# Router steps moved to the beginning of the pair two further on, and the residual additions of attention made by GpSimd, in a cross-attention and mixture-of-experts kernel

## The chip, the cores and the metric

The kernel runs on one core of one Trainium2 chip. Its time is the device time of one execution in microseconds (us). Three runs of the kernel before gave 643.98, 644.26 and 647.44 us; the median is 644.26 us. One more execution was profiled: 646.02 us, of which 644.2 us is the span from the first to the last instruction.

A core has five engines, each of which works through its own list of instructions in order: TensorE (PE), VectorE (DVE), ScalarE (ACT), GpSimd (POOL) and SyncE (SP, which here only starts DMAs). They wait for one another by semaphores. An instruction that waits holds back everything behind it on its engine.

## What is computed

```python
# 16 sequences of 128 tokens, width 256, 16 heads of 16
x = x + xattn(layernorm(x), ctx, ctx, pad_mask, causal_mask, Wq, Wk, Wv)
x = x + ffn(layernorm(x))

def ffn(x):                                   # 2048 tokens
    ys = geglu(x @ Ws1 + bs1) @ Ws2 + bs2     # shared expert, all tokens
    logits = (x @ Wr + br) / 1.5              # router, 12 experts
    top_val, top_idx = top_k(logits, 2)       # two experts for each token
    w = softmax(top_val)
    yr = sum over the two of w * (geglu(x @ We1[e] + be1[e]) @ We2[e] + be2[e])
    return ys + yr
```

## The kernel before

**Two phases.** The 16 sequences are treated in 8 pairs (0 to 7); the attention of these pairs fills the first 200 us or so. Then come the shared expert and the routed experts, in 43 slots of 128 tokens. Between them GpSimd scatters the normalised tokens to the rows of their experts (`scatter`, 32 indirect DMAs, two for each of 16 token tiles) and converts the first expert's weights.

**A pair on TensorE.** For each of a pair's two sequences (b = 0, 1) there is one *score burst* (`scores`, lines 568 and 574: the mask, then q times k), which fills the PSUM tile `ps_s`. The burst of sequence 0 of pair p+1 stands at the end of pair p (`next_scores`), that of sequence 1 in the middle of a pair. VectorE takes every burst in two halves ("units"): a maximum (`softmax_max`, line 1317), then a subtraction out of `ps_s` (`softmax_add`, line 1324). The next burst waits until all units of the one before are subtracted (`shifted`). ScalarE makes the exponentials, TensorE transposes them in four groups per sequence (`prob_transposes`, line 585), ScalarE copies each group, and TensorE multiplies by the values (`values`, line 595). Then ScalarE copies the result (`out_copy`), TensorE transposes it back (`out_transposes`, line 603), and VectorE divides it (`norm`, into the tile `att`) and adds it to `x_all` (`residual`, line 1348). `residual` also takes the statistics of the second layer norm.

**Steps.** Between these pieces stand the *steps* of other pairs, each of which goes through one of two PSUM banks in turn (`ps_x` and a half of `ps_t`): `k`, `q`, `v` (the projections of the next pair), `xT` (transposes of the normalised x two pairs on), `r` and `l` (the router of pair p-1: transposes of the second layer norm's output `xn2p`, line 488, and the product with the router's weights, line 539), and `n` (the ranks of tokens within their experts, for the first 8 tiles). The steps have one numbering over all pairs (`order`, `index_of`); a step on TensorE waits until the one two before it is taken out of its bank (`xb_free`), and `l` waits until ScalarE has copied `r`. VectorE makes the low halves of `k`, `q` and `xT` and takes out `l`.

**The second layer norm.** After the residual of sequence 1, GpSimd computes 1/sqrt of the variance (`rstd`), VectorE makes `xn2p` (`ln2_apply`, line 1364), SyncE saves it (`save_xn2`), and TensorE's step `r` reads it, all of it in the pair after the one that it belongs to.

**GpSimd** normalises x for pair p+2 (`normalise_x`), splits the context for pair p+2 into two parts (`split_ctx`), and in pairs 1 to 4 converts the shared expert's weights. **SyncE** loads the context, saves `xn2p` and fills the rows of the experts with zeros (`fill`, 8 DMAs of 3.3 MB). The scatters wait for all fills, for `xn2p` of the first four pairs and for the row numbers of the first 8 tiles (`rows_ready`).

**Line numbers** are those of the kernel before. The rows of the changed kernel in the section on the change have its own numbering (line 585 has become 595, and so on).

Of the kernel before, what the change touches and what calls it, by code (L numbers as in the profile page):

```python
# [18 lines left out]
B, S, D = 16, 128, 256  # L19
# [33 lines left out]
def build(nc, x_d, ctx_d, pad_d, sub_d, wq_d, wk_d, wv_d, bias_d, bst_d, tab_d, ws1_d, ws2_d, w1_d,  # L53
# [260 lines left out]
    def order(p, first, last):  # L314

        if last:
            return ["r", "l", "n"]
        if first:
            return ["xT", "k", "q", "v", "xT"]
        if isinstance(p, int) and p == PAIRS - 2:  # L320
            return ["k", "q", "n", "v", "r", "l"]
        return ["k", "q", "v", "xT", "r", "l"]

    def base_of(p, first):

        return len(FIRST) if first else 6 * p + len(FIRST) - 1
# [15 lines left out]
    def each_pair(eng, body):  # L342

        body(0, 0, True, False)
        with eng.Fori(0, (PAIRS - 4) // 2) as i:
            body(i * 2 + 1, 1, False, False)
            body(i * 2 + 2, 0, False, False)
        body(PAIRS - 3, 1, False, False)
        body(PAIRS - 2, 0, False, False)
        body(PAIRS - 1, 1, False, True)  # L350
# [23 lines left out]
    with block:  # L374
# [3 lines left out]
        def _(sp):  # L378
# [50 lines left out]
            def pair(p, first):  # L429

                sp.wait_ge(c_split, p + 2)
                load_ctx(p + 2)
                if not first:
                    save_xn2(p - 1)
                fill(p + 1)
# [4 lines left out]
            sp.wait_ge(c_split, PAIRS - 1)  # L440
            load_ctx(PAIRS - 1)
# [41 lines left out]
        def _(pe):  # L483
# [180 lines left out]
            def pair(p, par, first, last):  # L664
# [5 lines left out]
                def put(s, parts=(0, 1), again=False):  # L670

                    if s not in todo:
                        return
                    idx, bank = index_of(s, p, first, last, again), bank_of(s, p, first, last, again)
                    if s == "n":
                        rank_step(idx, bank, batch_in(p))
                    elif s in ("r", "l"):
                        router(s, p - 1, idx, bank, index_of("r", p, first, last) + 1)
                    else:
                        step(s, p + (2 if s == "xT" and (again or not first) else 1), 1 - par, idx, bank, parts=parts)  # L680
# [15 lines left out]
                else:  # L696
                    prev = p * 2 - 1
                    prob_transposes(prev, 0)
                    put("k", (0,))
                    prob_transposes(prev, 1)  # L700
# [11 lines left out]
                    put("n")  # L712
# [238 lines left out]
        def _(sc):  # L951
# [82 lines left out]
            def pair(p, par, first, last):  # L1034
# [5 lines left out]
                def put(s, again=False):  # L1040
# [4 lines left out]
                    if s == "r":  # L1045
                        router(s, idx, bank)
                    else:
                        step(s, 1 - par, idx, bank)
# [7 lines left out]
                else:  # L1056
                    prev = p * 2 - 1
                    prob_copy(prev, 0)
# [4 lines left out]
                    exp(p * 4, 0)  # L1063
                    out_copy(prev)
                    put("q")
# [6 lines left out]
                put("xT", first)  # L1072
                prob_copy(cur, 3)
                put("r")
# [4 lines left out]
                exp(p * 4 + 3, 3)  # L1079

# [127 lines left out]
        def _(ve):  # L1208
# [125 lines left out]
            def norm(p, b):  # L1334
# [4 lines left out]
                ve.wait_ge(nstep, (p * 2 + b) * 2 + 1)  # L1339
                vec.tensor_tensor(att[:, :].rearrange("p (h d) -> p h d", d=HD), o[:, :, 0:HD],  # L1340
# [3 lines left out]
            def residual(p, b):  # L1344
# [3 lines left out]
                vec.tensor_tensor(xs, xs, att[:, :], ALU.add).then_inc(added, 1)  # L1348
                ve.wait_ge(added, p * 2 + b + 1)
# [101 lines left out]
            def pair(p, par, first, last):  # L1451
# [5 lines left out]
                def put(s, again=False):  # L1457
# [6 lines left out]
                    elif s in ("r", "l"):  # L1464
                        router(s, p - 1, idx, bank)
# [13 lines left out]
                else:  # L1479
                    softmax_add(p * 4, 0)  # L1480
# [8 lines left out]
                    put("q")  # L1489
# [7 lines left out]
                softmax_max(p * 4 + 3, 3, p * 2 + 1)  # L1497
                if not first:
                    ln2_apply(p - 1)
                softmax_add(p * 4 + 3, 3)  # L1500
                put("xT", first)
                norm(p, 0)
                residual(p, 0)
                if first:
                    ve.wait_ge(x_rest_in, 16)
                    ve.wait_ge(router_in, 32)
                    ln1_stats(3)
                put("l")
                softmax_max(p * 4 + 4, 0, p * 2 + 2)
                if isinstance(p, int) and p == PAIRS - 3:  # L1510
                    choose(1, 0)
# [285 lines left out]
        def _(gp):  # L1797
# [55 lines left out]

            def first_step(s, q):
# [63 lines left out]
            split_ctx(2)  # L1918
            for p in range(1, PAIRS - 1):
# [11 lines left out]
                if p == 4:  # L1931
# [3 lines left out]
                    load_raw2(0)  # L1935

# [149 lines left out]
```

## Time and profile before

| | |
|---|---|
| median of three runs | 644.26 us |
| profiled execution | 646.02 us |
| its span | 644.2 us |
| PE busy | 582.1 us (90% of the span) |
| DVE busy | 447.1 us (69%) |
| ACT busy | 282.6 us (44%) |
| POOL busy | 364.5 us (57%) |
| mean granted TensorE clock | 0.954 of full speed |

Busy shares are averages over both phases. In the rows of the section further down, times are us from the span's start; a timeline row gives start, duration, engine, line, operation, output and inputs, and in brackets the idle time before it with the engine and line that ended it. The granted clock is given as a share of 2.4 GHz; it has two levels, 1.00 and 0.50.

### The profile page before, as it was taken

To read this page: it belongs to the slowest core of one execution; us is meant where nothing else is said; L and a number is where in the kernel's file an instruction comes from. 1 tells how busy PE (TensorE), PEld (TensorE's weight loads), DVE (VectorE), ACT (ScalarE), POOL (GpSimd) and SP (SyncE) were. 2 spreads that over 40 slices of the span, in tenths; PEclk is the share of its full clock that TensorE was granted. 3 is DMA by queue.
4 is the path that set the end of the run, shared out by engine and by line. 5 is a ranking of instruction groups with operands and counts; after the bars stand their busy time and mean duration, and the time that the engine had idled before them with its cause. 6 is when DMAs were issued, how large, how long until landed. Compare 5 with 4: busy or idle time off the path is not lost.

```text
span 644.2 us, 14068 instructions
## 1 busy us (share of the span) xinstructions
PE 582.1 (90%) x4092; PEld 479.8 (74%) x4093; DVE 447.1 (69%) x976; ACT 282.6 (44%) x629; POOL 364.5 (57%) x419
## 2 busy tenths in 40 slices
PE   7597979879788778799999999999999999999995
PEld 6465757656556777587887888878887888889995
DVE  5588668577678867667766677766676776665767
ACT  3255536454356623344444444444444444444432
POOL 3533151452108878699983886778886684000773
PEclk9799879789799989799999999999999999999998
DMA  9940651628651432364535365263465241110443
GB/s 289 395 173 31 216 185 61 244 99 292 227 214 68 172 140 91 122 225 156 204 136 179 95 222 188 81 228 130 144 222 183 86 131 33 33 34 18 139 134 121
DMA packets 47620, 98.91 MB, mean 154 GB/s; under 512 B 4449, under 2 KB 23521, under 8 KB 47585
## 3 DMA queue, kind: packets, MB, share of 16 engines
q1 hardware_dynamic: 36192, 50.41, 22.5%
q0 software_dynamic: 10976, 47.72, 22.2%
q10 hardware_dynamic: 416, 0.33, 0.2%
q8 instruction: 21, 0.34, 0.2%
q14 instruction: 15, 0.11, 0.1%
HBM read 57.15 MB, written 39.19 MB: 150 GB/s over the span
## 4 chain that ended last, share of the span: by engine, by line
PE 72%; DVE 12%; issue 5%; POOL 5%; ACT 3%; SPq 2%; DMA 1%; DVEq 0%; ACTq 0%; POOLq 0%
PE ps_s L790 29%; PE ps_o L823 9%; PE ps_o L824 5%; PE ps_s L752 4%; PE ps_t L800 3%; PE ps_t L585 3%; PE ps_s L568 2%; POOL rows_in L1913 2%; PE ps_s L574 2%; DVE prob L1324 2%; PE ps_x L510 2%; PE ps_t L510 2%; DVE nmax L1317 1%; PE ps_s L800 1%; PE ps_x L539 1%
## 5 line engine op out<-in xcount | busy, mean ns | idle before, releaser
L790 PE MATMUL ps_s<-ring,xTh 128*128 (+1 forms) x516 | 153.4, 419 | 0.5 <-DVE xTl L1638 0.5
L790 PEld LDWEIGHTS ps_s<-ring,xTh 128*128 128x128 f32 x516 | 89.2, 191 | 14.6 <-DVE xTl L1638 0.8
L1624 DVE TENSOR_TENSOR ag<-ps_s,up_bias 128x512 f32<-128x512 f32 x129 | 89.1, 691 | 12.1 <-PE ps_s L790 7.4
L823 PE MATMUL ps_o<-ring,hTh 128*128 x258 | 96.0, 410 | 0.8 <-issue 0.8
L1814 POOL TENSOR_TENSOR ring<-stage,ring 128x512 fp32r<-128x512 f32 x76 | 95.7, 1292 | 1.1
L790 PE MATMUL ps_s<-ring,xTl 128*128 (+1 forms) x258 | 81.0, 395 | 0.0
L824 PE MATMUL ps_o<-ring,hTl 128*128 x258 | 72.3, 280 | 0.0
L1800 POOL TENSOR_TENSOR ve<-mv,eps 128x2 f32<-128x2 f32 x16 | 3.5, 216 | 116.9 <-DVE mv L1356 100.6
L2025 POOL DMA_INDIRECT gath<-rows_out,idx_out x32 | 31.0, 968 | 65.8 <-DMA rows_out<-y_row 56.3
L1629 DVE TENSOR_TENSOR ag<-ag,ps_s 128x256 f32<-128x256 f32 x129 | 54.3, 421 | 16.0 <-ACT ps_s L1105 0.5
L1105 ACT ACTIVATE ps_s<-ag 128x256 f32<-128x256 f32 x129 | 50.2, 389 | 32.4 <-DVE ag L1624 31.0
L980 ACT ACTIVATE probT<-ps_t 128x512 f32<-128x512 f32 x64 | 37.8, 597 | 52.4 <-PE ps_t L585 51.2
L790 PEld LDWEIGHTS ps_s<-ring,xTl 128*128 128x128 f32 x258 | 48.8, 189 | 11.4
L1113 ACT ACTIVATE hTh<-ps_t 128x256 fp32r<-128x256 f32 x86 | 33.1, 385 | 53.6 <-PE ps_t L800 53.6
L1647 DVE TENSOR_TENSOR y_row<-ps_o,y_lo 128x256 f32<-128x256 f32 x43 | 18.3, 425 | 55.0 <-ACT y_lo L1128 55.0
L823 PEld LDWEIGHTS ps_o<-ring,hTh 128*128 128x128 f32 x258 | 48.5, 188 | 10.6 <-issue 1.0
L1827 POOL TENSOR_TENSOR ring<-stage,ring 128x512 fp32r<-128x512 f32 x40 | 51.0, 1300 | 1.2
L1633 DVE TENSOR_TENSOR hTl<-ps_t,hTh 128x256 fp32r<-128x256 f32 x86 | 36.1, 420 | 21.5 <-issue 16.8
L824 PEld LDWEIGHTS ps_o<-ring,hTl 128*128 128x128 f32 x258 | 48.9, 189 | 0.0
L1324 DVE TENSOR_TENSOR prob<-ps_s,nmax 128x1024 f32<-128x1024 f32 x32 | 39.1, 1221 | 13.2 <-PE ps_t L585 12.9
L752 PE MATMUL ps_s<-xgh,ring 128*128 128x256 f32 x256 | 47.4, 292 | 0.3
L1317 DVE TENSOR_REDUCE nmax<-ps_s 128x8 f32<-128x1024 f32 x32 | 38.9, 1217 | 10.3 <-PE ps_s L574 8.7
(254 smaller groups left out, 1290.1 us busy)
## 6 DMA issues: line engine op xcount, KB each, us to landing
rows_in<-y_row SPq DMA_DIRECT2D x8, 3328.0 KB, 13.7
stage<-in_w POOLq DMA_DIRECT2D x12, 1536.0 KB
stage<-in_w POOLq DMA_DIRECT2D x12, 768.0 KB, 5.4
up_bias<-in_bias POOLq DMA_DIRECT2D x12, 768.0 KB, 5.1
xrow<-rows_in SPq DMA_DIRECT2D x43, 128.0 KB, 2.2
rows_out<-y_row SPq DMA_DIRECT2D x43, 128.0 KB, 1.8
c_raw<-in_ctx SPq DMA_DIRECT2D x8, 256.0 KB, 10.7
xn_all<-xn2p SPq DMA_DIRECT2D x8, 256.0 KB, 2.6
```

Of the source, the lines that this page charges most:

```text
L752: last = pe_.matmul(ps_s[:, c, half * D:(half + 1) * D], weights(place, off + k * 2 * HS + half * D + col, P), x[:, k, :], start=n == 0, s ...
L790: last = pe_.matmul(ps_s[:, i, :], x[:, c, :], weights(place, off + c * 2 * HR + i * 2 * D, 2 * D), start=n == 0, stop=n == 5)
L823: pe_.matmul(ps_o[:, :], hTh[i][:, c, :], weights(place, a, 2 * D), start=i == 0 and c == 0, stop=False)
L824: pe_.matmul(ps_o[:, 0:D], hTl[i][:, c, :], weights(place, a, D), start=False, stop=False)
L980: act.activation(probT[:, g, :, :], ps_t[:, bank, :].rearrange("p (j t) -> p j t", j=4), ACT.Identity).then_inc(pt_copied, 1)
L1105: act.activation(ps_s[:, i, D:2 * D], ag[i][:, 1, :], ACT.Gelu).then_inc(gelu_done[i], 1)
L1317: vec.tensor_reduce(nmax[:, :, :], group_scores(n), AX.X, ALU.max, negate=True).then_inc(maxed, 1)
L1324: vec.tensor_tensor(prob[n % 2][:, :, :, :].rearrange("p a j t -> p j a t"), src, nmax[:, :, :].rearrange("p j (a o) -> p j a o", o=1).bro ...
L1624: vec.tensor_tensor(ag[i][:, :, :].rearrange("p a n -> p (a n)"), ps_s[:, i, :], bias, ALU.add)\
L1629: vec.tensor_tensor(ag[i][:, 0, :], ag[i][:, 0, :], ps_s[:, i, D:2 * D], ALU.mult).then_inc(hid_done[i], 1)
L1814: last = pool.tensor_tensor(lo_ap[:, c:c + PIECE], src[:, c:c + PIECE], hi_ap[:, c:c + PIECE].bitcast(f32), ALU.subtract)
L1827: last = pool.tensor_tensor(both[:, c:c + 2, 1, :], raw[:, c:c + 2, :], both[:, c:c + 2, 0, :].bitcast(f32), ALU.subtract)
```

## The change

Four things are changed, all in the attention phase.

1. The router steps `r` and `l` of pair p-2 (before: p-1) stand at the beginning of pair p (before: at the end). The last two pairs whose router is still in the loop go together into pair 6: its list is `r, l` (pair 4), `k, q, v, n, R, L` (`R`, `L` are the router of pair 5). `n` moves from the middle of pair 6 to its end.
2. `xT` is put behind the last transposes of the probabilities on TensorE and behind `out_copy` on ScalarE; VectorE applies the second layer norm after the last subtraction of a pair, not before it, and the low half of `k` before the second subtraction, not after it. ScalarE copies q before the result.
3. The addition `x_all + att` is made by GpSimd for 13 of the 16 sequences (both of pairs 0 to 5, and the first of pair 6). VectorE keeps the statistics (`ln2_stats`) and waits for `added`; GpSimd waits for `normed`. On GpSimd `normalise_x` moves behind `split_ctx` and the weights' conversion, since the statistics that it needs (`ln1_stats(p+2)`) are now taken in pair p.
4. The context for pair p+3 is loaded in pair p behind the saving of `xn2p` and ahead of the fill; before, the load for p+2 stood ahead of both, and came behind the previous pair's fill.

```diff
@@ order
         if isinstance(p, int) and p == PAIRS - 2:
-            return ["k", "q", "n", "v", "r", "l"]
-        return ["k", "q", "v", "xT", "r", "l"]
+            return ["r", "l", "k", "q", "v", "n", "R", "L"]
+        return ["r", "l", "k", "q", "v", "xT"]
...
@@ SyncE, pair
                 else:
                     save_xn2(p - 1)
+                    sp.wait_ge(c_split, p + 3)
+                    load_ctx(p + 3)
                     fill(p + 1)
...
@@ TensorE, pair
                 cur = p * 2
...
                 values(0, par, cur, (1,))
-                put("xT", again=first)
                 prob_transposes(cur, 3)
                 values(0, par, cur, (2,))
-                put("r")
+                put("xT", again=first)
                 values(0, par, cur, (3,))
-                put("l")
                 out_transposes(cur)
+                put("n")
                 next_scores()
+                if "R" in todo:
+                    put("R")
+                    pe.wait_ge(xb_free, index_of("L", p, first, last) - 1)
+                    spin(3, step_bank[bank_of("L", p, first, last)][:, 0:D])
+                    put("L")
...
@@ VectorE, pair
                 else:
+                    put("l")
                     softmax_add(p * 4, 0)
-                    softmax_shift(p * 4 + 1, 1, p * 2)
+                    softmax_max(p * 4 + 1, 1, p * 2)
                     put("k")
-                    if isinstance(p, int) and p == PAIRS - 3:
+                    softmax_add(p * 4 + 1, 1)
...
+                    if isinstance(p, int) and p == PAIRS - 2:
                         choose(0, 0)
-                    elif not isinstance(p, int):
-                        ln1_stats(p + 3)
+                    else:
+                        ln1_stats(p + 2)
+                    put("q")
                     softmax_max(p * 4 + 2, 2, p * 2 + 1)
                     norm(p - 1, 1)
-                    put("q")
+                if isinstance(p, int) and p == PAIRS - 2:
+                    choose(1, 0)
                 softmax_add(p * 4 + 2, 2)
                 if not first:
-                    residual(p - 1, 1)
+                    ln2_stats(p - 1, 1)
+                softmax_max(p * 4 + 3, 3, p * 2 + 1)
+                softmax_add(p * 4 + 3, 3)
+                if not first:
+                    ln2_apply(p - 1)
+                put("xT", first)
...
@@ GpSimd
+            def residual(p, b):
+
+                gp.wait_ge(normed, p * 2 + b + 1)
+                xs = x_all[:, (p * 2 + b) * D:(p * 2 + b + 1) * D]
+                pool.tensor_tensor(xs, xs, att[:, :], ALU.add).then_inc(added, 1)
+
...
             for p in range(1, PAIRS - 1):
-                if p + 2 < PAIRS:
-                    normalise_x(p + 2)
-                rstd(ln2_var, ln2_rs, mv2, ve2, rs2, p - 1, pstep2)
                 if p + 2 < PAIRS:
                     split_ctx(p + 2)
...
+                if p + 2 < PAIRS:
+                    normalise_x(p + 2)
+                residual(p - 1, 1)
+                rstd(ln2_var, ln2_rs, mv2, ve2, rs2, p - 1, pstep2)
+                gp.wait_ge(xn2_ready, p)
+                residual(p, 0)
```

**TensorE in a pair of the loop.** Before, at the end of a pair: `ps_x<-const,xn_132` is `xT`, `ps_t<-const,xn2p` is `r`, `wr,xn2T` is `l`, `ps_t<-const,prob` a group of transposes, `probT,v_sb` the product with the values, `outT` the transposes back.

```order
L488 MATMUL ps_x<-const,xn_132 128x128 x4
L583 REGISTER_ALU
L585 MATMUL ps_t<-const,prob_130 128x128 x4
L595 MATMUL ps_o<-probT,v_sb_128 32x128 x4
L532 REGISTER_ALU
L488 MATMUL ps_t<-const,xn2p 128x128 x4
L591 REGISTER_ALU
L595 MATMUL ps_o<-probT,v_sb_128 32x128 x4
L536 REGISTER_ALU
L539 MATMUL ps_x<-wr,xn2T 128x12 x4
L603 MATMUL ps_o<-const,outT 128x128 x4
```

Now, at the end of a pair:

```order
L595 MATMUL ps_t<-const,prob_130 128x128 x4
L605 MATMUL ps_o<-probT,v_sb_127 32x128 x4
L505 REGISTER_ALU
L508 REGISTER_ALU
L498 MATMUL ps_x<-const,xn_132 128x128 x4
L601 REGISTER_ALU
L605 MATMUL ps_o<-probT,v_sb_127 32x128 x4
L613 MATMUL ps_o<-const,outT 128x128 x4
```

and at the beginning of the next, right behind the score burst:

```order
L584 MATMUL ps_s<-km_lo_126,q_hi_118 128x256 x4
L542 REGISTER_ALU
L498 MATMUL ps_t<-const,xn2p 128x128 x4
L591 ISA
L593 REGISTER_ALU
L595 MATMUL ps_t<-const,prob_129 128x128 x4
L505 REGISTER_ALU
L520 MATMUL ps_t<-cTh_113,wkh 128x256 x2
L520 MATMUL ps_t<-cTl_115,wkh 128x256 x2
L520 MATMUL ps_t<-cTh_113,wkl 128x256 x2
L525 MATMUL ps_t<-sel_k,bias_tab 128x256
L549 MATMUL ps_x<-wr,xn2T 128x12 x4
```

Both router steps have gone from between the last transposes and `outT` to behind the score burst, with the first group of transposes and half of `k` between them.

**GpSimd, a pass of its loop (pair 2 or so).** Before (`xn_132` is the normalised x, `ve_73`, `rs_74` the second layer norm's 1/sqrt, `cTh`, `cTl` the split context, `ring` the shared expert's weights):

```order
L1800 TENSOR_TENSOR ve_69<-mv_68,eps 128x2
L1802 TENSOR_TENSOR rs_70<-ve_69,half 128x2
L1850 TENSOR_SCALAR xn_132<-x_all,mv_68,rs_70 128x256 x2
L1800 TENSOR_TENSOR ve_73<-mv_72,eps 128x2
L1802 TENSOR_TENSOR rs_74<-ve_73,half 128x2
L1839 TENSOR_SCALAR cTh_114<-c_raw 128x512
L1841 TENSOR_TENSOR cTl_116<-c_raw,cTh_114 128x512
L1882 TENSOR_TENSOR ring<-stage_85,ring 128x512 x2
```

Now:

```order
L1865 TENSOR_SCALAR cTh_114<-c_raw 128x512
L1867 TENSOR_TENSOR cTl_116<-c_raw,cTh_114 128x512
L1914 TENSOR_TENSOR ring<-stage_85,ring 128x512 x2
L1826 TENSOR_TENSOR ve_69<-mv_68,eps 128x2
L1828 TENSOR_TENSOR rs_70<-ve_69,half 128x2
L1876 TENSOR_SCALAR xn_132<-x_all,mv_68,rs_70 128x256 x2
L1884 TENSOR_TENSOR x_all<-x_all,att 128x256
L1826 TENSOR_TENSOR ve_73<-mv_72,eps 128x2
L1828 TENSOR_TENSOR rs_74<-ve_73,half 128x2
L1884 TENSOR_TENSOR x_all<-x_all,att 128x256
```

The split and the weights stand first, then the normalisation, and the two additions `x_all<-x_all,att` enclose the 1/sqrt of the second layer norm.

**VectorE in pair 6, from the statistics of pair 5 on.** Before (`pos` takes out the ranks, the six rows after it are the row numbers that the scatters wait for, the last of them sets `rows_ready`):

```order
L1350 MEMSET tick 128x1
L1351 BN_STATS bn_71<-x_all 128x6
L1354 MEMSET tick 128x1
L1356 BN_AGGR mv_72<-bn_71 128x2 x2
L1413 TENSOR_TENSOR pos<-ps_t,const 128x96
L1420 TENSOR_TENSOR eq<-pos,pick_154 128x96
L1421 TENSOR_REDUCE best<-eq 128x8
L1422 CAST idx_top<-best 128x8
L1420 TENSOR_TENSOR eq<-pos,pick_155 128x96
L1421 TENSOR_REDUCE best<-eq 128x8
L1422 CAST idx_top<-best 128x8
L1317 TENSOR_REDUCE nmax<-ps_s 128x8
L1364 TENSOR_SCALAR xn2p<-x_all,mv_72,rs_74 128x256 x2
```

Now, from the last subtraction of the pair on:

```order
L1342 TENSOR_TENSOR prob_130<-ps_s,nmax 128x4x2x128
L1389 TENSOR_SCALAR xn2p<-x_all,mv_72,rs_74 128x256 x2
L1438 TENSOR_TENSOR pos<-ps_x,const 128x96
L1445 TENSOR_TENSOR eq<-pos,pick_154 128x96
L1446 TENSOR_REDUCE best<-eq 128x8
L1447 CAST idx_top<-best 128x8
L1445 TENSOR_TENSOR eq<-pos,pick_155 128x96
L1446 TENSOR_REDUCE best<-eq 128x8
L1447 CAST idx_top<-best 128x8
L1356 RECIPROCAL rden<-ps_o 128x16
L1360 TENSOR_TENSOR att<-ps_o,rden 128x256
L1335 TENSOR_REDUCE nmax<-ps_s 128x8
```

The row numbers have moved behind the last subtraction and `xn2p`, ahead of the division (`rden`, `att`) for the first sequence of pair 6.

## Rows read from the trace of the kernel before

**Rows 1.** Waits from 17 to 230 us: total us, times, longest.

```profile
ACT xn2T L997 <- DVE xTl L1268: 17.5, 5, 3.7
...
PE ps_t L488 <- DVE xn2p L1364: 15.1, 7, 3.5
```

**Rows 2.** Windows: length, busy of PE, PEld, DVE, ACT, POOL, clock, DMA share, GB/s.

```profile
40.00:60.00 20.00, 18.58 (x214) 13.37 (x206) 17.73 (x37) 12.89 (x20) 4.71 (x7) 1.00 0.01 3
116.00:120.00 4.00, 3.68 (x15) 3.01 (x16) 0.68 (x2) 2.65 (x4) 3.47 (x5) 0.50 1.02 380
```

**Rows 3.** Timeline of PE at the end of pair 0.

```profile
40.53 0.42 PE L595 MATMUL ps_o<-probT,v_sb 128*32 128x128 f32 x8 [0.33 <-ACT probT L980]
...
42.23 1.03 PE L568 MATMUL ps_s<-mask_b,ident_b 128*128 128x512 bf16 x4
```

**Rows 4.** Timeline of PE, pair 4 of the attention.

```profile
121.69 0.66 PE L585 MATMUL ps_t<-const,prob 128*128 128x128 f32 x4
...
129.32 1.04 PE L568 MATMUL ps_s<-mask_b,ident_b 128*128 x4
...
139.38 0.63 PE L488 MATMUL ps_t<-const,xn2p 128*128 128x128 f32 x4 [2.06 <-DVE xn2p L1364]
...
141.70 1.88 PE L539 MATMUL ps_x<-wr,xn2T 128*128 128x12 f32 x8 [1.34 <-ACT xn2T L997]
```

**Rows 5.** Timeline of DVE, pair 4.

```profile
127.69 1.23 DVE L1324 TENSOR_TENSOR prob<-ps_s,nmax 128x1024 f32<-128x1024 f32 x1 [1.33 <-PE ps_t L585]
...
131.31 1.23 DVE L1317 TENSOR_REDUCE nmax<-ps_s 128x8 f32<-128x1024 f32 x1
...
137.26 1.96 DVE L1364 TENSOR_SCALAR xn2p<-x_all,mv,rs 128x256 f32 x2
...
140.28 0.68 DVE L1268 TENSOR_TENSOR xTl<-ps_x,xTh 128x512 fp32r<-128x512 f32 x1
```

**Rows 6.** Groups of instructions up to 250 us: count, busy us, mean ns, idle before.

```profile
L1850 POOL TENSOR_SCALAR xn<-x_all,mv,rs 128x256 f32<-128x256 f32 x14 | 17.0, 1224 | 0.8
...
L1802 POOL TENSOR_TENSOR rs<-ve,half 128x2 f32<-128x2 f32 x16 | 11.7, 730 | 1.3
...
L1841 POOL TENSOR_TENSOR cTl<-c_raw,cTh 128x512 fp32r<-128x512 f32 x8 | 10.1, 1265 | 0.7
...
L1348 DVE TENSOR_TENSOR x_all<-x_all,att 128x256 f32<-128x256 f32 (+1 forms) x16 | 7.2, 450 | 0.8 <-DVE att L1340 0.2
```

**Rows 7.** The tile c_raw: the eight context loads, from issue to landing.

```profile
DMA to landing us min/median/max: 3.6/10.7/18.6
```

**Rows 8.** DMA issues: count, KB each, median us to landing.

```profile
xn_all<-xn2p SPq DMA_DIRECT2D x8, 256.0 KB, 2.6
```

**Rows 9.** Timeline of SP: the last two fills.

```profile
166.82 2.98 SPq L417 DMA_DIRECT2D rows_in<-y_row  x2
```

**Rows 10.** Window in which the last fills end.

```profile
184.00:188.00 4.00, 2.76 (x46) 2.37 (x39) 2.41 (x4) 1.45 (x2) 0.00 (x0) 1.00 0.55 206
```

**Rows 11.** Timeline of PE: the score burst that opens pair 6.

```profile
171.32 1.91 PE L568 MATMUL ps_s<-mask_b,ident_b 128*128 128x512 bf16 x4
```

**Rows 12.** Timeline of DVE, pairs 5 and 6.

```profile
156.42 0.20 DVE L1380 TENSOR_SCALAR lg<-logits 128x96 f32<-128x96 f32 x1
...
158.40 1.22 DVE L1317 TENSOR_REDUCE nmax<-ps_s 128x8 f32<-128x1024 f32 x1
...
191.05 0.23 DVE L1413 TENSOR_TENSOR pos<-ps_t,const 128x96 f32<-128x96 f32 x1
...
193.90 0.73 DVE L1364 TENSOR_SCALAR xn2p<-x_all,mv,rs 128x256 f32<-128x256 f32 x2
```

**Rows 13.** Timeline of POOL: the first scatter.

```profile
193.86 1.12 POOL L1913 DMA_INDIRECT rows_in<-xn_all,idx_top  x1 [1.69 <-PE ps_t L585]
```

**Rows 14.** Timeline of DVE: the last second layer norm.

```profile
225.96 0.74 DVE L1364 TENSOR_SCALAR xn2p<-x_all,mv,rs 128x256 f32<-128x256 f32 x2 [2.29 <-POOL rs L1802]
```

**Rows 15.** Window within the expert phase, columns as in rows 2.

```profile
300.00:400.00 100.00, 99.10 (x525) 82.13 (x524) 67.95 (x147) 43.65 (x120) 78.76 (x91) 1.00 0.51 171
```

More of the change, by code:

```diff
@@ L319, in order @@
             return ["xT", "k", "q", "v", "xT"]
+        if isinstance(p, int) and p == 1:
+            return ["k", "q", "v", "xT"]
         if isinstance(p, int) and p == PAIRS - 2:
-            return ["k", "q", "n", "v", "r", "l"]
-        return ["k", "q", "v", "xT", "r", "l"]
+            return ["r", "l", "k", "q", "v", "n", "R", "L"]
+        return ["r", "l", "k", "q", "v", "xT"]
     def base_of(p, first):
-        return len(FIRST) if first else 6 * p + len(FIRST) - 1
+        if first:
+            return len(FIRST)
+        if isinstance(p, int) and p in (1, PAIRS - 1):
+            return len(FIRST) + 5 if p == 1 else base_of(PAIRS - 2, False) + 8
+        return 6 * p + len(FIRST) - 3
     def index_of(s, p, first, last, again=False):
@@ L429, in pair @@
             def pair(p, first):
-                sp.wait_ge(c_split, p + 2)
-                load_ctx(p + 2)
-                if not first:
+                if first:
+                    sp.wait_ge(c_split, 2)
+                    load_ctx(2)
+                    fill(1)
+                    sp.wait_ge(c_split, 3)
+                    load_ctx(3)
+                else:
                     save_xn2(p - 1)
-                fill(p + 1)
+                    sp.wait_ge(c_split, p + 3)
+                    load_ctx(p + 3)
+                    fill(p + 1)
             pair(0, True)
@@ L677, in put @@
                     elif s in ("r", "l"):
-                        router(s, p - 1, idx, bank, index_of("r", p, first, last) + 1)
+                        router(s, p - 2, idx, bank, index_of("r", p, first, last) + 1)
+                    elif s in ("R", "L"):
+                        router(s.lower(), p - 1, idx, bank, index_of("R", p, first, last) + 1)
                     else:
@@ L1044, in put @@
                     idx, bank = index_of(s, p, first, last, again), bank_of(s, p, first, last, again)
-                    if s == "r":
-                        router(s, idx, bank)
+                    if s in ("r", "R"):
+                        router("r", idx, bank)
                     else:
@@ L1057, in pair @@
                     prev = p * 2 - 1
+                    put("r")
                     prob_copy(prev, 0)
@@ L1071, in pair @@
                 prob_copy(cur, 2)
-                put("xT", first)
                 prob_copy(cur, 3)
-                put("r")
                 if first:
@@ L1339, in norm @@
                 ve.wait_ge(nstep, (p * 2 + b) * 2 + 1)
+                if not (isinstance(p, int) and p == 0 and b == 0):
+                    ve.wait_ge(added, p * 2 + b)
                 vec.tensor_tensor(att[:, :].rearrange("p (h d) -> p h d", d=HD), o[:, :, 0:HD],
@@ L1348, in residual, with ln2_stats @@
                 vec.tensor_tensor(xs, xs, att[:, :], ALU.add).then_inc(added, 1)
+                ln2_stats(p, b)
+            def ln2_stats(p, b):
+                xs = x_all[:, bass.ds((p * 2 + b) * D, D)]
                 ve.wait_ge(added, p * 2 + b + 1)
@@ L1463, in put @@
                         rank_step(idx, bank, batch_in(p))
-                    elif s in ("r", "l"):
-                        router(s, p - 1, idx, bank)
+                    elif s in ("l", "L"):
+                        router("l", p - (2 if s == "l" else 1), idx, bank)
                     else:
@@ L1496, in pair @@
                     row_numbers(0)
[L1497 to L1501, printed above, removed]
-                norm(p, 0)
[L1503 to L1508, printed above, removed]
+                norm(p, 0)
                 softmax_max(p * 4 + 4, 0, p * 2 + 2)
-                if isinstance(p, int) and p == PAIRS - 3:
-                    choose(1, 0)
+                ln2_stats(p, 0)
+                put("L")
             each_pair(ve, pair)
```

18 lines of the change are left out of this document (12 added, 6 removed).

## Prediction

> **What bounds the kernel now.** I first look where the time is bound by what the change touches. Behind the attention TensorE works without a break: 99.10 us of 100 at full clock [rows 15]. Nothing there is touched, so that phase starts earlier or later as a whole. What counts is when it may start.
>
> Next the waits of the attention phase [rows 1]. TensorE waited 7 times, 15.1 us in all, for `xn2p` before the router's transposes, and ScalarE waited 17.5 us to copy these out, because the shared step numbering makes that copy wait for the low half of `xT`.
>
> The timeline of one pair shows how this falls on the path [rows 4]. In pair 4 TensorE's first transposes start at 121.69 and its second score burst at 129.32. It has nothing to do from 137.32 (139.38 less its wait of 2.06) until `xn2p` is there, and then waits 1.34 more for ScalarE's copy. The clock pays too: 1.00 from 40 to 60 us, where no router step stood in the way, but 0.50 from 116 to 120 [rows 2], behind the same wait one pair earlier. The router's product took 1.88 us there [rows 4].
>
> Last, how the attention hands over. The chain of waits leaves TensorE at the first scatter, at 193.86 [rows 13], and runs through GpSimd, which scatters and converts without a gap. The last `xn2p` waits 2.29 us for GpSimd [rows 14]. So the hand-over is as early as GpSimd's first scatter is. My sum is the time of that scatter.
>
> **The change, part by part.** I count from the start of the first score burst of a pair (its zero).
>
> *TensorE in a pair.* The work is the same, in another place. The burst takes 2.0 (129.32 to VectorE's maximum at 131.31) [rows 4, 5]. The router's transposes take 0.55 (0.63 less the overlap of about 0.1), the first half 7.6 (121.69 to 129.32), the router's product 0.94 (half of 1.88, at full clock) [rows 4]. Second burst at 11.1. From it to 137.32 are 8.0 [rows 4]; `xT` is in it. From the last product with the values to the next burst were 1.70 in pair 0 (40.53 to 42.23), with ScalarE's copy waited for, since no router step stood between [rows 3]. That wait stays; before, the router hid it. Sum 20.8. `xn2p` is now a pair old, its wait gone.
>
> *VectorE in a pair.* From the maximum at 131.31 to `xTl` at 140.28 are 8.97 without a gap [rows 5]. Out of it go `xn2p` 1.96 [rows 5], the addition 0.45 [rows 6], and the low half of q, about 0.65: 5.9 left. The maximum starts at 13.1, so the last subtraction ends at 19.0, and TensorE asks at 20.8 or a little before: 1.8 spare. The first half: the second subtraction waited 1.33 for TensorE's transposes [rows 5], and the low half of k (1.3) now fills just that wait. If it did not, TensorE would lose up to 1.3 a pair. I take 0.2, for copies that come late.
>
> *GpSimd in a pair.* An addition is not shown. The nearest row is the split, 1.265 for 512 columns, so 0.63 for 256; the upper bound is the normalisation, 1.22 for 256 columns [rows 6]; below, VectorE's own 0.45 [rows 6]. I take 0.65. The statistics of layer norm 1 end near 11.7; then 0.93 for the root, 2.45 for the normalisation and 0.65 for the addition bring GpSimd to 15.8 [rows 6]. VectorE asks at 16.3 (13.1, 1.15, 0.65, its subtraction held until TensorE's transposes at 15.2). Spare 0.5, or none at 1.22. The other addition, at 1 to 2, is asked for at 3. So the additions cost nothing while GpSimd is on time; nor do they gain, since VectorE has 1.8 over.
>
> The row for contention: `xn2p` took 1.96 where GpSimd was busy with the split [rows 5], 0.73 at 193.90 where it only started scatters [rows 12]. The Trainium skill, SBUF — State Buffer, "Who interferes with whom", says that VectorE and GpSimd lock a shared port pair against each other, but not for a VectorE instruction with at most one SBUF input outside the 2-port modes. By that rule the moved normalisation and additions cost VectorE nothing, for the maxima and subtractions beside them read PSUM, and `xn2p`, now beside an idle GpSimd, gets faster. If the lock held for every instruction, up to 2.4 a pair would be added to VectorE, of which 0.6 would show. The trace agrees as far as these rows go: the instruction that the rule names was 1.96 against 0.73.
>
> *Pair 6.* Its zero was 171.32 [rows 11], the first scatter came 22.5 later. Now `choose(0, 0)` adds 2.0 (156.42 to 158.40) [rows 12] less the 1.0 of the statistics, under which the maximum starts at 13.2; `choose(1, 0)` adds 1.7 (six such instructions). The last subtraction ends at 13.2 + 5.9 + 1.7 = 20.8. Behind it stand `xn2p` 0.75, the row numbers 1.8 (seven small instructions from 191.05) [rows 12], the division 0.65; on GpSimd, which has the last addition ahead of the scatters, 0.65; and 0.5 until the scatter. First scatter at 25.2: 2.7 later in its pair than before. The fills don't hold it: issued at 166.82, four us before the pair's zero, they ended near 186.2 (window at 0.55 of DMA) [rows 9, 10], 19.4 after their issue. Now they are issued at about 0.7 and end at 20.1; at their median of 13.7 each alone they would end at 28 and cost 3.
>
> *The sum.* Pair 1 starts at 42.2 as before [rows 3]. It has no router steps: 20.8 - 1.5 = 19.3. Four pairs of 20.8 + 0.2 make 84.0. Pair 6 starts at 145.5, before at 171.32: 25.8 gained. The first scatter comes at 170.7, before at 193.86: **23.2 gained**. TensorE is ready earlier than that by some us, and waits for GpSimd in the last pair. Against the profiled 646.02 this makes 622.8; that execution lies 1.76 above the median of the runs, so against 644.26 it is **621.1 us**.
>
> **The rivals.**
>
> *The clock still falls in each pair.* For it: waits of 0.8 remain for `out_copy`. Against it: pairs 0 and 1 had such waits (0.33 before the last values [rows 3]) at clock 1.00 [rows 2]. A fall like that from 116 to 120 costs 2 us (4 at half speed): six pairs, 12 us. Time 633. The Trainium skill, TensorE: Matmul & The Clock Gate, on a second failure mode, tells of a kernel in which many short waits between groups of matmuls made the clock swing; by that the fall would come although no wait is long.
>
> *GpSimd comes late.* Its list is now a ring: split, weights, normalisation, addition; VectorE's statistics, root and `xn2p` hang on the end. The ring starts with the context load, issued behind the saving of `xn2p` at about 0.9. If it lands at L, the pair lasts L + 1.9 (split) + c (weights, 0 to 5.7, 13 over pairs 1 to 5) + 4.1 (root, normalisation, addition) + 3.1 (statistics, a unit, the burst) = L + c + 9.1. I take L = 4.5: 3.6 is the shortest landing [rows 7], 2.6 the median of a saving as large [rows 8]; then only pair 4 is late, by under 1. At the median 10.7 [rows 7], which was behind a fill, the five pairs last 113 us where the sum above has 103: gain 13, time 631.
>
> *The same, but slower than before.* The five pairs lasted 129.1 us (42.23 to 171.32), and the scatter has to make up 2.7. From L = 13.6 on (5 L + 58.6 = 126.4) the kernel is slower; at the longest landing, 18.6 [rows 7], by 25 us: 669. For it: the context load now is held until `xn2p` is saved, which ties one ring to the other. Against it: it is ahead of the fill, not behind one, and 18.6 was read among the loads of the start.
>
> **How the numbers follow.** Forecast 0.82 (616 to 627 by itself: additions, copies and hops each off by a few tenths in every pair, the fills at 28), clock 0.06, GpSimd late but faster 0.07, slower 0.03; 0.02 for gains that the hand-over loses down to nothing. The range 616 to 631 leaves out the last two and half of the clock's case. A difference of 0.5% is about what a measurement of this kernel tells from none: faster by more 0.95, within it 0.02, slower 0.03.
>
> **What would show it.** The first bursts of pairs 2 to 6 some 21 us apart (before 25 to 27); no idle time of TensorE for `xn2p` in them and one of 0.8 before each `outT`; clock 1.00 from 40 to 165 us; the first scatter near 171; the last but one `xn2p` waiting for GpSimd's root, which before it hardly did. It is wrong if TensorE waits for `xn1` or VectorE for `x_all` of GpSimd in each pair, if the fills release the first scatter, or if the pairs get shorter and the first scatter does not follow.

## The result, and the profile after

| | before | after |
|---|---|---|
| median of the runs, us | 645.85 (4 runs, 643.98 to 647.59) | 628.17 (4 runs, 627.03 to 628.43) |
| profiled execution, us (span) | 646.02 (644.2) | 628.38 (626.4) |
| first scatter on GpSimd, us | 193.86 [rows 13] | 174.77 |
| mean granted clock of TensorE | 0.954 | 0.968 |

The changed kernel takes 0.9723 of the time of the kernel before, with a 95% interval of 0.9685 to 0.9762: 17.7 us less. The forecast was 621.1 us, 23.2 less than 644.26, with a range of 616 to 631. It named the right case, and the gain came out 5.5 us too large.

I read the profile after in the same order. First TensorE's waits, from 17 to 230 us.

```profile
PE ps_o L613 <- ACT outT L1002: 5.1, 7, 0.8
PE ps_t L595 <- ACT probT L997: 3.7, 9, 0.5
PE ps_x L498 <- POOL xn L1876: 3.7, 1, 3.7
PE ps_x L498 <- DVE xn2p L1389: 3.6, 1, 3.6
...
PE ps_t L498 <- DVE xn2p L1389: 2.1, 1, 2.1
```

Of the seven waits for `xn2p` [rows 1] two are left, and both lie in the hand-over. What remains in a pair is ScalarE's copies. Then the windows (columns as in rows 2).

```profile
32.00:36.00 4.00, 3.34 (x33) 2.46 (x34) 2.39 (x3) 1.54 (x2) 2.21 (x3) 0.73 1.05 410
36.00:40.00 4.00, 4.00 (x39) 3.34 (x38) 3.79 (x4) 1.80 (x4) 0.00 (x0) 0.85 0.82 313
40.00:60.00 20.00, 18.56 (x214) 13.38 (x206) 15.10 (x29) 12.50 (x20) 9.21 (x13) 1.00 0.01 2
60.00:168.00 108.00, 99.92 (x1098) 73.86 (x1102) 82.67 (x161) 64.17 (x101) 43.00 (x53) 1.00 0.63 232
...
196.00:200.00 4.00, 4.00 (x42) 3.45 (x42) 3.52 (x18) 2.49 (x4) 3.09 (x4) 0.50 0.94 290
236.00:240.00 4.00, 3.17 (x18) 2.64 (x16) 3.28 (x12) 2.27 (x4) 2.52 (x2) 0.67 0.23 26
```

The clock is 1.00 through pairs 1 to 5, where it was 0.50 from 116 to 120 before [rows 2]. It is low in pair 0 and in the hand-over. The bursts that open pairs 1, 3 and 6, and the end of a pair, on TensorE's timeline:

```profile
43.81 1.03 PE L578 MATMUL ps_s<-mask_b,ident_b 128*128 128x512 bf16 x4
...
84.99 1.03 PE L578 MATMUL ps_s<-mask_b,ident_b 128*128 x4
...
103.18 0.66 PE L595 MATMUL ps_t<-const,prob 128*128 128x128 f32 x4 [0.41 <-ACT probT L997]
103.77 0.42 PE L605 MATMUL ps_o<-probT,v_sb 128*32 128x128 f32 x8
104.12 0.66 PE L498 MATMUL ps_x<-const,xn 128*128 128x128 f32 x4
104.71 0.43 PE L605 MATMUL ps_o<-probT,v_sb 128*32 128x128 f32 x8
105.85 0.66 PE L613 MATMUL ps_o<-const,outT 128*128 128x128 f32 x4 [0.72 <-ACT outT L1002]
...
149.14 1.03 PE L578 MATMUL ps_s<-mask_b,ident_b 128*128 x4
```

Pair 1 starts at 43.81 (42.23 before [rows 3]) and lasts 19.73; the next four last 21.45, 21.35, 21.45 and 21.35; pair 6 starts at 149.14 (171.32 before [rows 11]). The context loads land sooner (min, median, max of `c_raw`, to compare with rows 7):

```profile
DMA to landing us min/median/max: 2.8/3.1/10.8
```

Last, GpSimd from the last addition in pair 6 through the hand-over, and below it VectorE's two last second layer norms.

```profile
173.81 0.73 POOL L1884 TENSOR_TENSOR x_all<-x_all,att 128x256 f32<-128x256 f32 x1 [4.46 <-DVE att L1360]
174.77 1.12 POOL L1945 DMA_INDIRECT rows_in<-xn_all,idx_top  x1 [0.24 <-issue]
...
192.48 0.72 POOL L1828 TENSOR_TENSOR rs<-ve,half 128x2 f32<-128x2 f32 x1
...
206.35 0.72 POOL L1828 TENSOR_TENSOR rs<-ve,half 128x2 f32<-128x2 f32 x1
...
245.68 0.57 POOL L1993 DMA_DIRECT2D up_bias<-in_bias  x1 [6.86 <-DVE idx_out L1559]
```

```profile
193.24 1.68 DVE L1389 TENSOR_SCALAR xn2p<-x_all,mv,rs 128x256 f32<-128x256 f32 x2 [4.39 <-POOL rs L1828]
...
207.11 0.74 DVE L1389 TENSOR_SCALAR xn2p<-x_all,mv,rs 128x256 f32<-128x256 f32 x2 [0.89 <-POOL rs L1828]
```

The *root* of a pair is GpSimd's 1/sqrt for its second layer norm (line 1828); `idx_out` are the row numbers by which the experts' results are gathered, and VectorE makes them when the last router product is in. I had called the hand-over as early as the first scatter. These rows cast doubt on it: VectorE now waits 4.39 us for the root of pair 6, and at 245 GpSimd, for all its unbroken scatters, waits 6.86 us for VectorE's `idx_out` (5.62 before). So two theories went into the experiments. *Scatter*: the first scatter sets the end. *Chain*: what sets it is the chain root of pair 6, `xn2p`, TensorE, root of pair 7, `xn2p`, routing, `idx_out`.

### The profile page after: what moved, and what is told of

Its sections match the earlier page's. It is cut to its first block, busy times and chain, and to the rows that moved or that the text cites. A ratio compares the mean times of both kernels' runs of the same rounds, so it can differ in the third digit from the quotient of the medians.

```text
span 626.4 us, 14101 instructions
## 1 busy us (share of the span) xinstructions
PE 575.7 (92%) x4098; PEld 477.0 (76%) x4099; DVE 436.6 (70%) x963; ACT 282.2 (45%) x629; POOL 374.6 (60%) x432
## 4 chain that ended last, share of the span: by engine, by line
PE 76%; DVE 8%; POOL 5%; issue 4%; ACT 4%; SPq 2%; DMA 1%; ACTq 0%; DVEq 0%; POOLq 0%
PE ps_s L807 30%; PE ps_o L840 10%; PE ps_o L841 5%; PE ps_s L769 4%; PE ps_t L595 3%; PE ps_t L817 3%; PE ps_o L605 2%; POOL rows_in L1945 2%; PE ps_s L584 2%; PE ps_s L578 2%; PE ps_t L520 2%; PE ps_t L532 2%; PE ps_s L817 1%; PE ps_x L828 1%; PE ps_x L520 1%
## 5 line engine op out<-in xcount | busy, mean ns | idle before, releaser
L1659 DVE TENSOR_TENSOR hTl<-ps_t,hTh 128x256 fp32r<-128x256 f32 x86 | 36.1, 419 | 21.4 <-issue 16.7
L769 PE MATMUL ps_s<-xgh,ring 128*128 128x256 f32 x256 | 48.8, 298 | 0.3
L1335 DVE TENSOR_REDUCE nmax<-ps_s 128x8 f32<-128x1024 f32 x32 | 38.9, 1216 | 10.2 <-PE ps_s L584 9.3
L1834 POOL TENSOR_SCALAR ring<-stage 128x512 fp32r<-128x512 f32 x76 | 45.0, 619 | 0.4
L595 PE MATMUL ps_t<-const,prob 128*128 128x128 f32 x256 | 39.7, 281 | 5.7 <-ACT probT L997 3.7
```

What stands on the lines that cost most here:

```text
L595: last = pe_.transpose(ps_t[:, bank, j * P:(j + 1) * P], prob[g // 2][:, g % 2, j, :], ident)
L769: last = pe_.matmul(ps_s[:, c, half * D:(half + 1) * D], weights(place, off + k * 2 * HS + half * D + col, P), x[:, k, :], start=n == 0, s ...
L1335: vec.tensor_reduce(nmax[:, :, :], group_scores(n), AX.X, ALU.max, negate=True).then_inc(maxed, 1)
L1834: last = pool.tensor_scalar(hi_ap[:, c:c + PIECE], src[:, c:c + PIECE], 1.0, 0.0, ALU.mult, ALU.add)
```

## The experiments

Each kernel differs from the changed one as its diff shows. Kernels of a group ran on the same chip beside runs of the kernel before; in groups one and three that one took 646.72 and 646.95 us, in group two 675.21. The last three columns are times of one traced execution each.

| group | kernel | median us | of before, 95% interval | first scatter | root of pair 7 | span |
|---|---|---|---|---|---|---|
| 1 | again | 626.64 | 0.9692 [0.9669, 0.9716] | 174.63 | 206.06 | 624.4 |
| 1 | xt_between | 626.33 | 0.9692 [0.9669, 0.9716] | 172.90 | 204.27 | 623.3 |
| 1 | res_vector | 626.76 | 0.9701 [0.9673, 0.9729] | 172.69 | 204.03 | 623.8 |
| 1 | late_scatter | 627.97 | 0.9710 [0.9685, 0.9735] | 176.45 | 207.80 | 625.3 |
| 2 | roots_early | 654.14 | 0.9685 [0.9636, 0.9734] | 174.83 | 208.87 | 651.7 |
| 2 | choose_early | 655.35 | 0.9695 [0.9643, 0.9748] | 176.47 | 211.49 | 653.5 |
| 2 | ctx_behind_fill | 670.44 | 0.9923 [0.9892, 0.9954] | 193.25 | 228.34 | 666.2 |
| 2 | warm | 651.60 | 0.9659 [0.9608, 0.9709] | 175.02 | 210.21 | 648.6 |
| 3 | again_b | 627.27 | 0.9693 [0.9676, 0.9709] | 174.81 | 206.11 | 625.8 |
| 3 | roots_early_b | 625.11 | 0.9655 [0.9637, 0.9674] | 175.02 | 204.15 | 622.8 |
| 3 | warm_four | 625.79 | 0.9674 [0.9654, 0.9695] | 174.14 | 205.58 | 623.2 |
| 3 | all_four | 622.52 | 0.9618 [0.9603, 0.9634] | 170.94 | 200.12 | 620.7 |

**The changed kernel again.** No edit.

> The changed kernel again, as the yardstick of the runs beside it. Both theories: ratio to the kernel before 0.972, and in the trace the first scatter near 174.8 us and the bursts of pairs 1 and 2 near 43.8 and 63.5; if the slow clock at 32 to 40 us was an accident of one execution, pair 1 starts near 42.2 here.

Pair 1 started at 43.70 and, in again_b, at 43.95. The first scatter is the same within 0.2 in three executions (174.77, 174.63, 174.81), but the rest of the span is not: 451.6, 449.8 and 451.0 us. A loss or gain of under 2 us behind the scatter can't be read from one trace.

**The additions on VectorE** (the order alone).

```
 gpsimd, pairs:  -residual(0, 0)
                 -residual(p - 1, 1)
                 -gp.wait_ge(xn2_ready, p); residual(p, 0)
 vector, pair:   -ln2_stats(p - 1, 1)      +residual(p - 1, 1)
                 -ln2_stats(p, 0)          +residual(p, 0)
```

> The residual additions on VectorE again, just ahead of their statistics; the new order kept. Theory (the order alone made the gain, VectorE has spare time): bursts still 21.4 us apart; the first scatter is no longer behind GpSimd's last addition (0.73 and two hops) but VectorE has 0.45 more ahead of it, so it comes near 174 (0.8 earlier), time 0 to 1 us under the changed kernel. Rival (the relief of VectorE is part of the gain): two additions of 0.45 in each pair come through, 0.9 x 6 = 5.4 us slower than the changed kernel.

The time is that of the kernel beside it: the moved additions bring nothing, so the gain comes from the other parts of the change. Pairs 2 to 5 are as long as in the run beside it within 0.02. Pair 6 reaches its first scatter 25.05 after its start instead of 25.63. The rest of the 1.9 is TensorE's clock in pair 0, below.

**xT between the groups again**, on TensorE (shown) and in the same way on ScalarE.

```
 prob_transposes(cur, 2); values(0, par, cur, (1,))
+put("xT", again=first)
 prob_transposes(cur, 3); values(0, par, cur, (2,))
-put("xT", again=first)
```

> TensorE transposes for xT between the third and fourth group of probability transposes again, and ScalarE copies it there (one part of the change undone, in pair 0 too). Theory: the 0.41 us that TensorE waits per pair for the copy of the third group, and part of the 1.6 us by which pair 1 starts late, come from this move; 6 x 0.4 plus up to 1.2 gives 2.4 to 3.6 us off the changed kernel, first scatter near 172. Rival: the wait only moves to the copy of outT, which is asked for that much earlier; time as the changed kernel within 0.5 us.

Between the two theories. The wait of 0.41 became one of 0.34 one step later, and a pair is 0.18 shorter (five pairs 104.38 us instead of 105.30), not 0.4. Pair 0's second burst was 0.7 early (31.78 instead of 32.52) before the edit comes into play. The time is the same.

Both kernels are also a test of the two theories, and neither comes out well. In the traces of res_vector and xt_between the first scatter came 1.9 and 1.7 earlier than in again and the root of pair 7 2.0 and 1.8, yet `idx_out` let GpSimd go on at 242.36 and 242.51, hardly before the 242.66 of again, and the spans are 0.6 and 1.1 shorter. The medians (0.1 longer and 0.3 shorter) need not show all of the lead: 1.3 and 0.9 of it came from pair 0 in the traced execution.

**The scatter later**, by four idle copies on GpSimd ahead of it.

```
+for late in (xn1, c_raw):
+    for b in range(2):
+        pool.tensor_scalar(late[:, b, :], x_all[...], 1.0, 0.0, ALU.mult, ALU.add)
 paced_scatters(range(3), (PAIRS - 2) * 8 + 1)
```

> Four idle GpSimd instructions of 256 columns (0.6 us each, 2.4 in all) ahead of the first scatter; they write to buffers that are done with. Theory (the first scatter sets the end, one to one): 2.4 us slower than the changed kernel, first scatter near 177.2. Rival (the hand-over hangs on TensorE or on xn2p of the last pairs, GpSimd has room): under 0.7 us slower.

The four took 0.38 each, not 0.6, and the scatter came 1.82 later; the span grew by 0.9, the median by 1.3. Both are more than the rival's 0.7, but the intervals of the medians overlap, and 0.9 between two traces is under the 2 us that can be read. The root of pair 7 moved by 1.74 too, so this does not tell scatter from chain.

**The context load behind the fill again.**

```
 save_xn2(p - 1)
+fill(p + 1)
 sp.wait_ge(c_split, p + 3)
 load_ctx(p + 3)
-fill(p + 1)
```

> The context load behind the fill again in pairs 1 to 5 (one part of the change undone). Theory: contexts then land near the 10.7 us of before instead of 3.1; GpSimd has 4.05 us of waiting for VectorE's statistics and 1.0 to 1.4 for the load in a pair, so by the formula of the forecast (landing + weights + 9.1, five pairs: 112 against 105) TensorE waits for xn1 or the split context and the time rises by 3 to 7 us. Rival: the fills leave the queue's way quickly enough or GpSimd's spare takes it; within 1 us of the changed kernel.

This moves two statements of the SP queue and takes back three quarters of the gain: 0.9923 against 0.966 to 0.970 of the three kernels beside it. The context lands at 11.1, near the 10.7 of the kernel before, GpSimd waits for it, and TensorE for GpSimd. The tile's line, then GpSimd's and TensorE's waits from 40 and 60 to 170 us, and two windows of pair 2:

```profile
DMA to landing us min/median/max: 3.5/11.1/12.2
```

```profile
POOL cTh L1865 <- DMA c_raw<-in_ctx: 44.6, 4, 11.9
```

```profile
PE ps_x L498 <- POOL xn L1876: 6.7, 3, 3.4
```

```profile
80.00:84.00 4.00, 2.07 (x27) 1.20 (x25) 0.14 (x1) 1.71 (x3) 3.82 (x5) 0.97 0.00 0
84.00:88.00 4.00, 2.82 (x16) 1.64 (x16) 2.64 (x7) 1.78 (x3) 2.01 (x4) 0.50 0.00 0
```

The pairs 1 to 5 last 19.7, 25.4, 26.6, 29.1 and 23.3 us, 124.1 in all, where my formula gives 5 x (11.1 + 9.1) + 13 = 114. It has no term for the clock, which falls behind the waits: of the 19 us by which these pairs are longer than in again, 6.7 are TensorE's wait for `xn`, and the mean clock from 60 to 170 us was 0.86. So "GpSimd comes late" was a real mechanism, and worse than I priced it; it did not come because the loads land at 3.1. The kernel before did not have it either: its loads landed as late as here, but GpSimd waited for none behind the second (its two waits for `c_raw` end at 4.38 and 18.59). So the order of the queue matters in the changed kernel; no run has it alone in the kernel before.

**The choice of experts earlier.**

```
 vector, end of pair 5:   +choose(0, 0)
 vector, pair 6, ahead of q's low half:    -choose(0, 0)   +choose(1, 0)
 vector, pair 6, behind norm(5, 1):        -choose(1, 0)
 each_pair: pairs 4 and 5 written out instead of in the loop
```

> The choice of the first expert for batch 0 at the end of pair 5 instead of inside pair 6, the second choice where the first stood; pairs 4 and 5 written out instead of looped. Both theories: first scatter 2.0 us earlier, near 172.7, if VectorE's spare 1.8 at the end of pair 5 takes the 2.0. Theory of the hand-over chain: all of GpSimd's roots come 2.0 earlier too, so 1.0 to 2.0 us under the changed kernel. Rival: VectorE is late in pair 6 by what it does not have, the scatter stays near 174.7, and the time with it.

Pair 1 began at 46.09, 2 us later than in its neighbours, so I count from pair 6's start: 25.16 to the scatter instead of 25.67 in roots_early. Only 0.5 of the 2.0 came through. On VectorE, in pair 6:

```profile
166.99 1.23 DVE L1344 TENSOR_TENSOR prob<-ps_s,nmax 128x1024 f32<-128x1024 f32 x1 [0.63 <-PE ps_t L597]
...
172.91 0.26 DVE L1440 TENSOR_TENSOR pos<-ps_x,const 128x96 f32<-128x96 f32 x1 [0.77 <-PE ps_x L565]
```

With the choices out of the way VectorE waits for TensorE's transposes and for its product with the ranks. Neither theory had that: TensorE stands right behind VectorE here.

**The two roots earlier.**

```
-if ahead_of_last and c + PIECE == n:
+if ahead_of_last and c + 3 * PIECE == n:
 ...
-for t in range(3, 7):
+for t in range(3, 6):
     scatter(t)
 rstd(ln2_var, ln2_rs, mv2, ve2, rs2, PAIRS - 1, pstep2)
+scatter(6)
 scatter(7)
```

> GpSimd makes the root of pair 6 two of its conversion pieces earlier and that of pair 7 one tile of scatters earlier; the number and order of its scatters stay. New theory (the end of the hand-over is a chain through xn2p of the last pairs, TensorE and VectorE to idx_out, for which GpSimd waits 4.3 to 6.9 us near 242): the root of pair 7 comes 2.5 us earlier and the time falls by about 2.5 us under the changed kernel. Rival (the first scatter sets the end, as the forecast had it, because GpSimd's stream behind it is the bound): no change, within 0.5 us.

> The two roots made earlier on GpSimd, again, beside a yardstick. Theory of the hand-over chain (VectorE waits for the roots of pairs 6 and 7, TensorE for VectorE, GpSimd at last for idx_out): root of pair 6 at 190, of pair 7 near 203.5 instead of 206, idx_out and the time 1.5 to 2.5 us earlier. Rival (GpSimd's scatter stream alone): no change within 0.5 us.

In group two this could not be read: on that chip TensorE stood still for 2 to 4 us near 181 and for about 5 near 200, ScalarE and VectorE with it, for no cause that the traces show, and the root of pair 7 waited 5.26 for VectorE. In group three it can: 625.11 against 627.27, intervals that don't touch. GpSimd's rows, with the `up_bias` issue at 242.09 instead of 244.05:

```profile
190.24 0.72 POOL L1828 TENSOR_TENSOR rs<-ve,half 128x2 f32<-128x2 f32 x1
...
204.15 0.72 POOL L1828 TENSOR_TENSOR rs<-ve,half 128x2 f32<-128x2 f32 x1
```

The first scatter came 0.2 later than in again_b, and the last one at 230.56 instead of 230.09, yet the time fell by 2.2 us, about as the root of pair 7 did (1.96). The scatter theory has no place for that; the chain through the roots has. It is one pair of kernels with five runs each, and res_vector and xt_between had the root as much earlier in their traces for little gain; so a root that comes earlier is worth something here, but not always its own size.

**Idle products in pair 0.**

```
 put("q")
+spin(9)        # warm;  spin(4) in warm_four
 scores(p, par, 1)
```

> Nine idle TensorE products ahead of the second score burst of pair 0, where TensorE waits 2.4 us for VectorE and the clock was 0.7 to 0.85 behind it in the changed kernel. Theory (the 1.3 us at the start of pair 1 is the clock, not the addition on GpSimd): clock 1.00 from 32 to 40 us, pair 1 at 42.4 instead of 43.7, time 1.3 us under the changed kernel. Rival (GpSimd's addition or the later xT make pair 1 late): pair 1 still at 43.7, no change.

> Four idle products ahead of the second burst of pair 0 (nine took 4.05 us at half clock and outlasted the wait they were to fill). Theory (the late start of pair 1 is the clock behind that wait): four end before VectorE is ready, clock 1.00 from 32 to 36 us, pair 1 at 42.4 instead of 43.7 and the time up to 1.3 us lower. Rival: the fall of the clock is older than the wait, or the late start has another cause; pair 1 at 43.7.

Nine took 4.05 us and outlasted the wait of 2.4; the burst came at 34.37. Four took 1.89, and TensorE still waited behind them:

```profile
33.41 1.04 PE L578 MATMUL ps_s<-mask_b,ident_b 128*128 128x512 bf16 x4 [1.45 <-DVE prob L1343]
```

The burst is 0.64 later than in again_b (32.77), but so was pair 0 ahead of the products (the transposes of `xT` at 24.96 instead of 24.32): the four cost nothing. Behind nine and behind four the clock was full; with four:

```profile
32.00:36.00 4.00, 2.59 (x34) 1.80 (x35) 2.39 (x4) 1.56 (x3) 2.97 (x3) 1.00 1.05 410
```

From that burst to pair 1's took 9.78 and 9.79, against 11.18 in again_b and 9.60 in the kernel before (32.63 to 42.23 [rows 3]). So 1.4 of the late start of pair 1 is the clock. In this trace 0.75 of it shows (43.20 instead of 43.95), since pair 0 was already 0.64 late ahead of the products. The medians differ by 1.5, with intervals that overlap.

**All four together**: additions on VectorE, xT between the groups, early roots, four idle products.

> Together: additions on VectorE, xT between the groups, both roots early, four idle products in pair 0. If the gains add up as the single runs showed (first scatter 1.9 earlier by the additions, 0.17 a pair by xT) and the hand-over chain follows: first scatter near 170.5, root of pair 7 near 200, time 3 to 5 us under the changed kernel. Rival (each gain is taken back at the hand-over, as it was for the first two alone): within 1 us of it.

622.52 us, 4.8 under again_b, with an interval clear of it. The root of pair 7 is at 200.12, 6.0 earlier than in again_b, and `idx_out` is waited for until 238.20 instead of 244.05. The span is 5.1 shorter, so 0.75 of that is lost behind it. It is the fastest version of this study, 3.8% under the kernel before.

## Why the prediction was right, and where it was off

*What bounds the kernel.* Right that the wait for `xn2p` ties TensorE up, twice over by the clock: with it gone the pairs went from 25.8 on average (129.1 over five) to 21.1, at clock 1.00. That the wait made the difference is read from the waits and the clock: res_vector and xt_between rule out two other parts of the change, but no run puts the router steps alone, or VectorE's new order alone, back.

*TensorE in a pair.* 20.8 + 0.2 was forecast, 21.4 measured; four pairs made 85.6, not 84.0. Also pair 1, 19.73 against 19.3. The first half took 11.2 (forecast 11.1), the second 10.2 (forecast 9.7). The step that was off is "The work is the same, in another place": where `xT` stood between the last two groups of transposes it covered ScalarE's copy, and now 0.41 of that shows in each pair, and 0.33 more before k, for the copy of `xn2T`. My 0.2 for copies was a third of the 0.6 that came. xt_between shows that putting `xT` back gains 0.18 only, since the copy is then waited for at the next product.

*Pair 1's start.* 42.2 was taken from a row of before, at clock 1.00. It came at 43.81. The runs show that as the clock in pair 0 (0.73 and 0.85 in this execution; 1.00 in the kernel before and in res_vector). What lets it fall in some kernels and not in others stays open: TensorE waited 2.4 to 2.6 us ahead of that burst in again and in res_vector alike.

*VectorE in a pair.* Right: `xn2p` took 0.73, the waits before the subtraction were 0.7 at most, and two additions of 0.45 put back cost nothing.

*GpSimd.* The addition took 0.735, between the bounds of 0.45 and 1.22, where I took 0.65. GpSimd was on time: no wait of TensorE for `xn1` in pairs 1 to 5. My L = 4.5 was 3.1. The Trainium skill, SBUF — State Buffer, "Who interferes with whom", was right about `xn2p`: 0.73 in the pairs, where GpSimd is idle, and 1.68 at 193.24, where GpSimd converts weights from 193.18 on. It also bears on a place that I had not looked at. Here VectorE compares two SBUF operands; in the changed kernel (first row) GpSimd adds from 164.44 on, in res_vector (second row) it is idle:

```profile
164.56 0.74 DVE L1407 TENSOR_TENSOR eq<-lg,top 128x96 f32<-128x96 f32 x1
```

```profile
163.05 0.26 DVE L1407 TENSOR_TENSOR eq<-lg,top 128x96 f32<-128x96 f32 x1
```

So the addition beside it costs VectorE 0.48 at this one instruction, on the way to the scatter. The rule names just this case, two SBUF inputs beside a GpSimd instruction that reads SBUF; I had weighed it for the maxima, the subtractions and `xn2p` alone.

*Pair 6.* 25.2 forecast, 25.63 measured, with the 0.48 in it. `xn2p` stood at 170.59 for 0.73, the row numbers ended at 173.05 and the addition at 174.54. The fills did not hold the scatter: the window from 168 to 172 has 0.14 of DMA.

*The sum up to the scatter.* Forecast 170.7, measured 174.77: 1.6 from pair 1's start, 0.4 from its length, 1.6 from the four pairs, 0.4 from pair 6 make 4.0 of the 4.1. All are terms of the sum that were sized too small.

*The hand-over.* This is the one step whose reason was wrong. "The hand-over is as early as GpSimd's first scatter is" held in size, but not for the reason given: root of pair 7 18.9 earlier than before, scatter 19.1, span 17.8. GpSimd hands out both the roots and the scatters in one stream, so the root moved with the scatter. With the roots alone moved, in roots_early_b, the time fell by 2.2 while the scatter stayed. The forecast had even named the wait of the last but one `xn2p` for its root as a sign to expect, and had drawn nothing from it. How far the root sets the end is open: from the root of pair 7 to the end of the wait for `idx_out` it was 39.3, 36.6 and 37.9 us in the three executions of the changed kernel and 38.2 in xt_between and 38.3 in res_vector, and no run shows why. What lay between 19.1 and 17.8 is not a property of the change either: it was 1.3 in this execution, and -0.6 and 0.6 in the two others, with the clock from 196 to 200 us at 0.50, 0.57 and 0.73.

*The rest of the difference.* 4.1 up to the scatter, 1.3 behind it and 0.1 outside the span are the 5.5 us of gain that did not come. With its fourth run the kernel before has a median of 645.85, not 644.26, which makes the 1.6 us more by which 628.17 misses 621.1.

*The rivals.* The clock did not fall in the pairs, though 1.5 us of short waits in each remained, so what the Trainium skill tells in TensorE: Matmul & The Clock Gate, "A second HAM failure mode", did not come about here; the trace shows 1.00 over 108 us with TensorE busy for 99.9. GpSimd late: ruled out for this kernel by the 3.1 of the loads, and shown to exist by one pair of statements. Two figures of this rival were wrong. 5 x (10.7 + 9.1) + 13 is 112, not 113, which moves its time to about 630. And the landing of 18.6 "was read among the loads of the start" is a misreading; it is that of the last load, issued 0.8 us behind a fill:

```profile
140.13 0.57 SPq L417 DMA_DIRECT2D rows_in<-y_row  x1
140.93 2.25 SPq L380 DMA_DIRECT2D c_raw<-in_ctx  x1
```

So only the other argument stood against the slow case, that the load is now ahead of the fill. It was right: the four loads from 64 to 128 us landed after 2.8 to 3.0.

## What to carry to other kernels

A step that hides behind nothing can often be done one stage later, when its input is old; count then what it had been covering, since a copy that it hid becomes a wait. When an engine hands out several results in one stream, ask which of them the end waits for: here, as far as the runs tell, it was not the first. Put the small load that a ring depends on ahead of the large one that nobody waits for; taking that order back cost three quarters of the gain here.

## What the runs showed of the hardware

A copy of 256 f32 columns on GpSimd took 0.38 us, an addition in place of 256 columns 0.735, a normalisation with two per-partition scalars 1.23: three prices for one size, where I had scaled one by columns. A small VectorE comparison of two SBUF operands went from 0.26 to 0.74 beside a GpSimd addition. And chips differ: in group two the kernel before took 675 us instead of 646. The traces of the changed versions there show pairs of the same length (warm: 85.5 us for the four that took 85.6), but TensorE standing still for 2 to 6 us at two places of the hand-over. That is a part of the difference only: in warm GpSimd's wait for `idx_out` ended 13 us later than in again_b, and 9.5 us more were lost behind it. The cause is open.
